# Layer 3 of a four-layer kernel on one core: delta path by channel, heads in pairs, a buffer for every group of fetched rows

## The chip, the core and the metric

The kernel runs on one core of a Trainium2 chip, as one program written by hand for five instruction streams: TensorE (PE), VectorE (DVE), ScalarE (ACT), GpSimd (POOL) and SyncE (SP), which wait for each other through semaphores. The metric is the device time of one execution in microseconds, the median of several runs. The order of each engine's instructions is what the program writes; nothing is reordered.

## What is computed

Four layers work on 4096 tokens of 128 channels (16 sequences of 256). In each, x = x + s * silu(m), where s is an attention-like part and m a feed-forward part of the normalised x. The change is in layer 3. Its s is a gated delta rule with short convolutions and three filters, four heads of 32 channels; its m is a mixture of eight experts, two for each token. Cut to what matters:

```python
b, l, d = hidden_states.shape                     # 16, 256, 128
q = _short_conv(hidden_states @ Wq.T, conv_q)     # k, v_direct alike; beta = sigmoid(h @ Wb.T)
# _delta_rule_chunkwise, chunks of 32 tokens, q and k normalised per head:
T = solve_triangular(eye - A, eye, lower=True)    # A = tril(-(kb @ k.T), -1)
u, w = T @ vc, T @ kbc
def step(S, inp):
    q_i, k_i, u_i, w_i = inp
    attn = jnp.where(causal, q_i @ k_i.T, 0.0)
    u_adj = u_i - w_i @ S
    return S + k_i.T @ u_adj, q_i @ S + attn @ u_adj
...
o = probs[..., 0:1] * local_s + probs[..., 1:2] * local_m + probs[..., 2:3] * local_l \
    + probs[..., 3:4] * delta_out + probs[..., 4:5] * v_direct
o = _rmsnorm(o, norm_w)
s = o.reshape(b, l, H * DV) @ Wo.T
# the experts: tokens are put into slots, 1280 for each expert; then
hid = gelu(a) * g                                 # a, g = halves of inp @ W_in
out_e = hid @ W_out
y = (out_pad[e_flat, l_flat].reshape(S, K, h) * gates[..., None]).sum(axis=1)
```

## The kernel before

All arrays of activations lie by channel (128 partitions) with the tokens along the free dimension; a *group* is 512 tokens (two sequences, four tiles of 128), and there are eight. All arithmetic is in float32. A call `mm(out, lhsT, rhs)` loads `lhsT` as weights, streams `rhs`, and writes `out` in one of eight PSUM banks; the trace shows two MATMUL records for each. The partitions of `lhsT` and `rhs` are the depth of the product, the width of `lhsT` is the number of output partitions, and the width of `rhs` the number of columns that stream. In the trace a form such as `128*32 128x128` reads: weights of 128 partitions and 32 columns, 128 columns streamed.

Layer 3 (`Layer3`, from L2356) has a first part (norm, routing, values, filters, scatter of the tokens into expert slots in DRAM, SyncE and GpSimd), and then four *quarters*, each of two groups (eight tiles). Every engine walks through the same numbered slots of a quarter, `L3_PERIOD` = 48 and two more in the last, and in each slot issues what is due:

- slots 0 to 3: u and w (`tensor_uw`, copied by `scalar_uw`, L3234), 16 products each, from the blocks of the inverse in `diag`, which SyncE has loaded (`sync_inverses`, L3197).
- slots 4 to 27: the recurrence over eight chunks, three slots each (`tensor_recur`): w @ S ("w"), q @ S into `b_o` ("o"), state update ("s"), four products each; VectorE subtracts after w (L3290) and masks the state after s (L3294). "w" of a chunk needs the state of VectorE, "s" needs its u.
- slots 28 to 36: eight heads (`tensor_heads`): in slot n the scores of head n into one of two banks, then the attention of head n - 1 on top of `b_o`; VectorE masks between (`vector_causal`, L3327), two buffers `s`.
- slots 35 to 45: two mixes (`*_mix`), one bank for both: VectorE multiplies the delta output by its gate (L3371), TensorE turns it ("turn", four transposes), VectorE adds it to the sum (L3377), ScalarE squares, TensorE averages, ScalarE takes Ln and Exp, VectorE scales (L3381), TensorE applies `Wo`, ScalarE copies.
- in quarters 0 to 2, beside it: the *front* of the next quarters (projections, convolution, norm, grams of q and k), the inverse of the next quarter on VectorE, one step a slot from slot 3 to 35 (`vector_invert`, L3177 to L3182), which SyncE stores and reloads from slot 37, and 14, 13 and 13 expert *units* of 256 slots: place (L2748), up (eight products 128x256, "a" and "g"), GELU on ScalarE, product on GpSimd (L2782), down.
- in quarter 3 no front and no units, but the *join*: GpSimd gathers the two expert rows of each token of a group (`gpsimd_gather`, L2811, eight indirect DMAs) into buffers of which there are two, multiplies the second half by its gate (`gpsimd_scale`, L2821), VectorE the first; TensorE adds and turns both (`tensor_join`, eight times two products with the identity), ScalarE applies SiLU (L2843), VectorE multiplies by s and adds to x (L2849, L2851). SyncE stores each group of x. Joins stand in slots 13, 17, ..., 41.

GpSimd's order in quarter 3 is gathers of groups 0 and 1, then for each group g: multiply g, gather g + 2; a gather waits for the join of the group that had the buffer before. TensorE's names in the trace: `weights_odd` and `weights_even` are two arenas of SBUF, `work` the third, `bank` is PSUM.

## Time and profile before

| | us |
|---|---|
| median of three runs | 3264.71 (3255.56 to 3266.56) |
| profiled execution | 3257.8 |
| its span | 3256.0 |
| TensorE busy (matmuls) | 2904.5 |
| VectorE, ScalarE, GpSimd busy | 1845.5, 1332.1, 1428.2 |
| layer 3, the four quarters, from the first u | 160.2, 162.0, 143.6, 150.6 |

A time of the profiled execution counts from the start of its span. Busy shares are averages over four layers with different limits. The quarters start at 2639.64, 2799.86, 2961.89 and 3105.40 us. The profile also gives the TensorE clock that was granted: 1.0 is 2.4 GHz, 0.5 is 1.2 GHz, and a mean lies between.

### The profile page before, as it was taken

What the parts mean: (1) busy time and instruction counts of PE and PEld (TensorE: products, weight loads), DVE (VectorE), ACT (ScalarE), POOL (GpSimd) and SP (SyncE); (2) the same over time, 40 slices, a digit from 0 to 9 for tenths busy, and PEclk for the clock granted to TensorE, in tenths of its full rate; (3) what the DMA queues carried; (4) which work ended last, traced back from release to release, by engine and by line L of the source; (5) the groups of instructions that cost most, each with busy time, mean ns of one, the idle gap of its engine ahead of it and who ended that gap; (6) DMA issues with size and microseconds to landing.
All of it is one profiled execution on the core that took longest, in us unless ns stands there. A gap on an engine that the chain in (4) does not pass through costs nothing.

```text
span 3256.0 us, 38772 instructions
## 1 busy us (share of the span) xinstructions
PE 2904.5 (89%) x13864; PEld 1786.7 (55%) x13864; DVE 1845.5 (57%) x3075; ACT 1332.1 (41%) x3233; POOL 1428.2 (44%) x1348
## 2 busy tenths in 40 slices
PE   6897799999999999799999999999788969898867
PEld 3564355555555555445555555444377857676756
DVE  6868577677677676466656565443442536252513
ACT  4452433433443443345555555443612323434311
POOL 3324366676676676267777777000003401010144
PEclk8997899999999999799999999999777768787876
DMA  5451100000000000420000000221121111111111
GB/s 187 159 177 55 50 1 1 1 1 1 1 1 1 1 1 1 102 63 15 1 1 1 1 1 1 66 75 56 40 82 59 56 35 41 46 36 48 37 39 46
DMA packets 160928, 128.88 MB, mean 40 GB/s; under 512 B 97688, under 2 KB 136864, under 8 KB 160224
## 3 DMA queue, kind: packets, MB, share of 16 engines
q1 hardware_dynamic: 148832, 90.13, 9.9%
q0 software_dynamic: 11904, 36.27, 3.5%
q8 instruction: 111, 1.82, 0.2%
q14 instruction: 81, 0.66, 0.1%
HBM read 105.70 MB, written 38.47 MB: 44 GB/s over the span
## 4 chain that ended last, share of the span: by engine, by line
PE 48%; ACT 4%; DVE 3%; issue 2%; POOL 1%; another core or an unknown queue 1%; SPq 0%; DMA 0%; DVEq 0%; ACTq 0%
PE bank L63 43%; PE bank L2051 4%; POOL weights_odd L2782 1%; SPq L3197 0%; ACT L3104 0%; DVE work L3179 0%; DVE work L3177 0%; DVE work L3136 0%; PE bank L2748 0%; PE bank L2901 0%; DVE weights_even L3136 0%; DVE work L1984 0%; ACT L3356 0%; POOL weights_odd L2811 0%
## 5 line engine op out<-in xcount | busy, mean ns | idle before, releaser
L63 PE MATMUL bank<-work 64*128 64x256 f32 (+5 forms) x4384 | 623.2, 356 | 16.9 <-DVE work L3294 3.9
L1491 POOL TENSOR_TENSOR work<-work 128x512 f32<-128x512 f32 x384 | 494.4, 1288 | 320.6 <-DVE work L1483 303.5
L63 PEld LDWEIGHTS bank<-work 64*128 64x128 f32 (+4 forms) x4384 | 444.6, 179 | 240.1 <-issue 135.6
L2039 POOL TENSOR_SCALAR work<-work 128x256 f32<-128x256 f32 x512 | 463.7, 922 | 242.2 <-DVE work L2030 242.0
L63 PE MATMUL bank<-weights_odd,normed_channels 128*128 128x512 f32 (+3 forms) x1152 | 524.8, 563 | 23.0 <-DVE work L1483 16.2
L63 PE MATMUL bank<-work,weights_even 128*32 128x128 f32 (+4 forms) x1136 | 326.3, 462 | 50.0 <-issue 10.6
L2024 ACT ACTIVATE work<-bank,work 128x256 f32<-128x256 f32 x512 | 236.8, 474 | 194.8 <-DVE work L2010 190.7
L1483 DVE TENSOR_TENSOR work<-bank,work 128x512 f32<-128x512 f32 x360 | 245.5, 686 | 110.0 <-PE bank L63 106.6
L63 PEld LDWEIGHTS bank<-weights_odd,normed_channels 128*128 128x128 f32 x1152 | 183.8, 195 | 161.1 <-issue 80.2
L63 PEld LDWEIGHTS bank<-work,weights_even 128*32 128x32 f32 (+4 forms) x1136 | 149.3, 180 | 184.0 <-issue 131.2
L2782 POOL TENSOR_TENSOR weights_odd<-weights_odd 128x512 f32<-128x512 f32 x40 | 51.5, 1288 | 445.1 <-ACT weights_odd L2777 445.1
L2010 DVE TENSOR_REDUCE work<-bank 128x2 f32<-128x512 f32 x256 | 164.9, 686 | 132.3 <-PE bank L63 132.3
L63 PE MATMUL bank<-work,weights_odd 128*128 128x512 f32 (+3 forms) x520 | 209.4, 519 | 25.5 <-ACT work L3355 6.6
L1558 ACT ACTIVATE work<-bank,work 128x256 f32<-128x256 f32 x256 | 119.6, 473 | 274.9 <-DVE work L1545 274.8
L63 PE MATMUL bank<-normed_channels,weights_even 128*128 128x512 f32 x432 | 230.5, 620 | 0.8 <-DVE work L1977 0.8
L63 PE MATMUL bank<-weights_even,work 128*128 128x128 f32 (+4 forms) x1152 | 176.1, 317 | 24.1 <-DMA work<-chunk_inverses 23.3
L2051 PEld LDWEIGHTS bank<-constants,work 128*128 128x128 f32 x1024 | 122.1, 141 | 123.9 <-issue 96.6
L63 PEld LDWEIGHTS bank<-weights_even,work 128*128 128x128 f32 (+2 forms) x1152 | 163.6, 221 | 41.1 <-DMA work<-chunk_inverses 23.7
L2695 POOL DMA_INDIRECT expert_rows_in<-weights_odd,expert_slots x64 | 63.7, 995 | 256.3 <-DVE expert_slots L2661 179.9
L63 PE MATMUL bank<-weights_odd 128*128 128x128 f32 (+3 forms) x664 | 149.8, 379 | 20.2 <-POOL weights_odd L2782 15.5
L1984 DVE TENSOR_SCALAR work<-bank,weights_even 128x512 f32<-128x512 f32 x128 | 96.1, 751 | 119.2 <-PE bank L63 119.2
L2051 PE MATMUL bank<-constants,work 128*128 128x128 f32 x1024 | 157.6, 276 | 2.3 <-DVE work L2059 1.1
(306 smaller groups left out, 4520.0 us busy)
## 6 DMA issues: line engine op xcount, KB each, us to landing
work<-gate_rows_L SPq DMA_DIRECT2D x64, 256.0 KB, 3.1
filter_matrices<-in_L_filters SPq DMA_DIRECT2D x24, 512.0 KB, 8.2
work<-filter_matrices SPq DMA_DIRECT2D x16, 768.0 KB, 4.2
expert_rows_in<-in_zeros SPq DMA_DIRECT2D x8, 640.0 KB, 11.2
weights_odd<-expert_rows_in SPq DMA_DIRECT2D x40, 128.0 KB
expert_rows_out<-weights_odd SPq DMA_DIRECT2D x40, 128.0 KB
weights_even<-expert_rows_in SPq DMA_DIRECT2D x20, 128.0 KB
expert_rows_out<-weights_even SPq DMA_DIRECT2D x20, 128.0 KB
```

What stands on the lines that cost most here:

```text
L63: return pe.matmul(out, lhsT, rhs, start=first, stop=last, skip_group_check=True)
L1483: v.tensor_tensor(heads(dst), heads(self.b_prod[p % 2][:, :]), self.per_head(self.score[g % 3], tile, kind == 0, e), ALU.mult).then_inc(s[ ...
L1491: gp.tensor_tensor(self.sum_of(p), self.sum_of(p), self.product_of(p), ALU.add).then_inc(s["l1_add"], 1)
L1558: a.activation(self.p[n % 2][:, c], self.b_score[n % 2][:, c], ACT.Exp, bias=self.mx[n % 4][:, i:i + 1], accum_out=self.sums(bt)[:, h, i:i ...
L1984: v.tensor_scalar(dst[n % 2], self.b_misc[:, :], bias[:, m:m + 1], scale, ALU.add, ALU.mult).then_inc(s["l2_qk"], 1)
L2010: v.tensor_reduce(self.mx[h % 8][:, 0:2], self.b_score[n % 2][half][:, :].rearrange("p (i j) -> p i j", j=SEQ), AX.X, ALU.max, negate=True ...
L2024: a.activation(self.p[h % 6][:, c], self.b_score[n % 2][half][:, c], ACT.Exp, bias=self.mx[h % 8][:, i:i + 1], accum_out=self.sums(n, half ...
L2039: gp.tensor_scalar(p[:, c], p[:, c], self.sums(n, half, i), None, ALU.mult).then_inc(s["l2_p"], 1)
L2051: last = pe.transpose(self.b_turn[:, jc * SEQ + i * P:jc * SEQ + (i + 1) * P], self.p[h % 6][:, i * SEQ + jc * P:i * SEQ + (jc + 1) * P], ...
L2695: gp.indirect_dma_start(self.k.x_rows[:, :], to, self.stage[g % 4][:, i * P:(i + 1) * P], None).then_inc(s[f"rows_moved{g % 4}"], 16)
L2782: gp.tensor_tensor(h, h, self.factor[n % 2], ALU.mult).then_inc(self.k.sem["moe_scaled"], 1)
```

## The change

1. **Delta path by channel, gate in the queries.** In the front, TensorE spreads the delta path's gate over the 32 channels of each head (16 products of a broadcast column with the identity) and VectorE multiplies the normalised q by it ("gated q"). "o" and the attention are written with operands swapped, so that `b_o` holds channels by tokens. VectorE's gate step and the transposes of the mix fall away.
2. **Heads in pairs.** In one slot the scores of two heads are issued in turn into two banks, then the attention of the two heads before; slots 28 to 32 instead of 28 to 36.
3. **Mixes in own banks**, with the states `S` as scratch, four slots each, in slots 31 to 36.
4. **Own buffers for the rows of each group.** Gathers wait only for the end of the expert units, for quarter 2's last scores, and for the rows of group g - 4 to have landed. The second multiplication goes to ScalarE, four ACTIVATEs. Joins stand at slots 8, 13, 18, 23, 28, 33, 37, 39; the last quarter has 42 slots, 8 fewer.

```diff
-L3_PERIOD = 48
+L3_PERIODS = (48, 48, 48, 42)
+L3_JOINS = (7, 12, 17, 22, 27, 32, 36, 38)
...
+        fetched = Arena(region.tensor, region.at, units_at).ring((region.at - units_at) // GW)
...
+        fetched = fetched[0:2 * (GROUPS - 3)] + [a[:, i * GW:(i + 1) * GW] for a in (*self.kk[1:3], q0) for i in range(2)]
+        self.rows = [fetched[2 * g:2 * g + 2] for g in range(GROUPS)]
+        self.b_mix = (b[3], b[4])
...
     def gpsimd_gather(self, gp, on, g):
-        if g >= 2:
-            self.moe_done(on, "moe_mm", MOE_MM, ("join", g - 2))
+        self.done(on, "l3_rec_mm", REC_MM, QUARTERS - 2, ("score", PAIRS - 1))
+        if g >= 4:
+            self.gathered(on, g - 4)
...
-    def gpsimd_scale(self, gp, on, g):
+    def scalar_scale(self, a, on, g):
         self.gathered(on, g)
-        gp.tensor_tensor(x, x, self.gates_of(1, g), ALU.mult).then_inc(self.k.sem["moe_scaled"], 1)
+        for i in range(TPG):
+            x, t = self.rows[g][1][:, i * P:(i + 1) * P], TPG * g + i
+            last = a.activation(x, x, ACT.Copy, scale=self.gate[1][:, t:t + 1])
+        last.then_inc(self.k.sem["moe_act"], 1)
...
+        if step == 5 and (g := self.front_of(n, 0)) is not None:
+            self.wait_front(on, "l3_front_dve", FRONT_DVE.index(("gated q", g)) + 1)
+            on.wait_ge(s["l3_probs"], 36)
+            for i in range(TPG):
+                for h in range(L3_H):
+                    last = mm(pe, b[h * L3_D:(h + 1) * L3_D, i * P:(i + 1) * P], self.path_gate(g, i, h), k.ident)
+            last.then_inc(done, 1)
...
+            v.tensor_tensor(dst, dst, self.b_front[:, :], ALU.mult).then_inc(done, 1)
...
-                last = mm(pe, o[r, i * P:(i + 1) * P], q[:, at:at + L3_CHUNK], S[:, b * P:(b + 1) * P],
-                          first=c < L3_CPT and b % BPG == 0, last=False)
+                last = mm(pe, o[:, i * P + r.start:i * P + r.stop], S[:, b * P:(b + 1) * P], q[:, at:at + L3_CHUNK],
+                          first=c == 0 and b % BPG == 0, last=False)
...
     def tensor_heads(self, pe, on, quarter, n):
             for i in range(TPG):
-                t = slice(at + i * P, at + (i + 1) * P)
-                last = mm(pe, self.b_head[n % 2][:, i * P:(i + 1) * P], kk[r, t], q[r, t])
+                for e in range(2):
+                    j, h = HEADS[2 * n + e]
+                    r, t = slice(h * L3_D, (h + 1) * L3_D), slice(j * GW + i * P, j * GW + (i + 1) * P)
+                    last = mm(pe, self.b_head[e][:, i * P:(i + 1) * P], kk[r, t], q[r, t])
             last.then_inc(done, 1)
...
-                last = mm(pe, self.b_o[j][:, d], self.s[(n - 1) % 2][:, i * P:(i + 1) * P],
-                          self.u[:, j * GW + d.start:j * GW + d.stop], first=False, last=True)
+                for e in range(2):
+                    j, h = HEADS[2 * n - 2 + e]
+                    r, t = slice(h * L3_D, (h + 1) * L3_D), slice(i * P, (i + 1) * P)
+                    last = mm(pe, self.b_o[j][r, t], self.u[:, j * GW + t.start + r.start:j * GW + t.start + r.stop],
+                              self.s[e][:, t], first=False, last=True)
...
     def gpsimd(self, gp, on):
-        for g in range(GROUPS + 2):
-            if g >= 2:
-                self.gpsimd_scale(gp, on, g - 2)
-            if g < GROUPS:
-                self.gpsimd_gather(gp, on, g)
+        for g in range(GROUPS):
+            self.gpsimd_gather(gp, on, g)
```

What this does to the order of the instructions, at three places. First TensorE in quarter 2 from slot 28. Of the kernel before: `128x128` from `weights_even,work` are scores, `128x32` the attention, the rows of `weights_odd` an expert unit (x counts the calls of `mm`):

```order
L63 MATMUL bank<-weights_odd 128x256 x4
L63 MATMUL bank<-weights_even,work 128x128 x8
L63 MATMUL bank<-work 128x32 x4
L63 MATMUL bank<-weights_odd 128x128 x4
L2748 MATMUL bank<-constants,weights_odd 128x128 x2
L63 MATMUL bank<-weights_even,work 128x128 x4
L63 MATMUL bank<-work 128x32 x4
L63 MATMUL bank<-weights_odd 128x256 x4
L63 MATMUL bank<-weights_even,work 128x128 x4
L63 MATMUL bank<-work 128x32 x4
L63 MATMUL bank<-weights_even,work 128x128 x4
```
And now (`32x128` is the attention):

```order
L63 MATMUL bank<-weights_odd 128x256 x4
L63 MATMUL bank<-weights_even,work 128x128 x16
L63 MATMUL bank<-work 32x128 x8
L63 MATMUL bank<-weights_odd 128x128 x4
L2765 MATMUL bank<-constants,weights_odd 128x128 x2
L63 MATMUL bank<-weights_even,work 128x128 x8
L63 MATMUL bank<-work 32x128 x8
L63 MATMUL bank<-weights_odd 128x256 x4
L63 MATMUL bank<-weights_even,work 128x128 x8
L63 MATMUL bank<-work 32x128 x16
L63 MATMUL bank<-work,weights_odd 128x512
```
Two heads stand where one stood, the scores of two pairs come first, and the mean of the first mix follows the last attention.

Second, TensorE in quarter 3 around the last recurrence step and the first heads. `constants,weights_odd 128x128 x8` is a join. Before:

```order
L63 MATMUL bank<-constants,weights_odd 128x128 x8
L63 MATMUL bank<-work 32x128 x4
L63 MATMUL bank<-work,weights_even 128x128 x8
L63 MATMUL bank<-work 128x32 x4
L63 MATMUL bank<-constants,weights_odd 128x128 x8
L63 MATMUL bank<-work,weights_even 128x128 x4
L63 MATMUL bank<-work 128x32 x4
L63 MATMUL bank<-work,weights_even 128x128 x4
L63 MATMUL bank<-work 128x32 x4
L63 MATMUL bank<-work,weights_even 128x128 x4
L63 MATMUL bank<-work 128x32 x4
L63 MATMUL bank<-work,weights_even 128x128 x4
```
And now, up to the last-but-one join (`work,weights_odd 128x512` are means and outputs of the mixes; `constants,work` and `constants,weights_even` are joins whose rows lie in the other arenas):

```order
L63 MATMUL bank<-work,weights_even 128x128 x8
L63 MATMUL bank<-constants,weights_odd 128x128 x8
L63 MATMUL bank<-work,weights_even 128x128 x8
L63 MATMUL bank<-work 32x128 x8
L63 MATMUL bank<-work,weights_even 128x128 x8
L63 MATMUL bank<-work 32x128 x8
L63 MATMUL bank<-work,weights_even 128x128 x8
L63 MATMUL bank<-work 32x128 x16
L63 MATMUL bank<-work,weights_odd 128x512
L63 MATMUL bank<-constants,work 128x128 x8
L63 MATMUL bank<-work,weights_odd 128x512 x3
L63 MATMUL bank<-constants,work 128x128 x8
```
The heads have moved together and the joins lie ahead of them and behind; before, three joins came after this place, each in front of two heads' work or of the mixes.

Third, GpSimd at the end of its stream. Before, with the expert products (L2782) ahead:

```order
L2782 TENSOR_TENSOR weights_odd<-weights_odd 128x512 x40
L2811 DMA weights_odd<-expert_rows_out,expert_slots 128x128 x16
L2821 TENSOR_TENSOR weights_odd<-weights_odd 128x512
L2811 DMA weights_odd<-expert_rows_out,expert_slots 128x128 x8
L2821 TENSOR_TENSOR weights_odd<-weights_odd 128x512
L2811 DMA weights_odd<-expert_rows_out,expert_slots 128x128 x8
```
And now:

```order
L2510 MEMSET work 128x4096
L2799 TENSOR_TENSOR weights_odd<-weights_odd 128x512 x40
L2829 DMA weights_odd<-expert_rows_out,expert_slots 128x128 x40
L2829 DMA work<-expert_rows_out,expert_slots 128x128 x16
L2829 DMA weights_even<-expert_rows_out,expert_slots 128x128 x8
```
The multiplications between the gathers are gone, and the gathers stand in one row.

## Rows read from the trace of the kernel before

**Rows 1.** Busy time by stretch: slots 28 to 47 of quarters 0 to 2, and quarter 3.
```profile
core 0: us, PE busy (x) PEld busy (x) DVE busy (x) ACT busy (x) POOL busy (x), PEclk, DMA share, GB/s
2734.03:2799.86 65.83, 52.73 (x270) 43.23 (x269) 24.24 (x30) 22.18 (x37) 8.85 (x7) 0.82 0.18 47
2898.41:2961.89 63.48, 52.88 (x252) 43.57 (x252) 24.21 (x30) 20.00 (x33) 7.60 (x6) 0.76 0.18 46
3042.14:3105.40 63.26, 52.75 (x251) 43.64 (x251) 24.70 (x31) 20.00 (x33) 7.58 (x6) 0.76 0.13 32
3105.40:3256.00 150.60, 103.14 (x585) 87.47 (x583) 36.99 (x52) 19.29 (x26) 70.50 (x72) 0.68 0.15 43
```

**Rows 2.** Timeline of TensorE, quarter 3: start, length, operation, count, idle before and releaser.
```profile
3134.83 3.62 PE L63 MATMUL bank<-work 128*32 128x128 f32 x16 [0.78 <-DVE work L3294]
...
3140.78 1.93 PE L63 MATMUL bank<-work 128*32 128x128 f32 x16 [0.78 <-DVE work L3294]
...
3144.58 1.06 PE L63 MATMUL bank<-work 128*32 128x128 f32 x8 [0.78 <-DVE work L3294]
3145.57 2.05 PE L63 MATMUL bank<-constants,weights_odd 128*128 128x128 f32 x16
...
3189.95 3.76 PE L63 MATMUL bank<-constants,weights_odd 128*128 128x128 f32 x16 [5.82 <-issue]
...
3204.89 3.76 PE L63 MATMUL bank<-constants,weights_odd 128*128 128x128 f32 x16 [7.10 <-issue]
...
3212.42 2.07 PE L63 MATMUL bank<-work,weights_even 32*128 32x128 f32 x8
3214.42 1.92 PE L63 MATMUL bank<-work 128*128 128x32 f32 x8
```

**Rows 3.** Timeline of GpSimd, quarter 3: gathers (L2811) and multiplication (L2821).
```profile
3193.98 0.98 POOL L2811 DMA_INDIRECT weights_odd<-expert_rows_out,expert_slots  x1 [4.13 <-PE bank L63]
...
3202.77 0.95 POOL L2811 DMA_INDIRECT weights_odd<-expert_rows_out,expert_slots  x1 [0.30 <-issue]
3203.73 1.06 POOL L2821 TENSOR_TENSOR weights_odd<-weights_odd 128x512 f32<-128x512 f32 x1
3208.92 0.99 POOL L2811 DMA_INDIRECT weights_odd<-expert_rows_out,expert_slots  x1 [4.13 <-PE bank L63]
```

**Rows 4.** Timeline of ScalarE: the second u copied (L3234) in quarters 2 and 3.
```profile
2974.53 0.60 ACT L3234 ACTIVATE work<-bank 128x512 f32<-128x512 f32 x1 [6.34 <-PE bank L63]
...
3129.78 0.60 ACT L3234 ACTIVATE work<-bank 128x512 f32<-128x512 f32 x1 [13.59 <-remote]
```

**Rows 5.** Timeline of TensorE, quarter 2: w, scores, attention, expert units.
```profile
2965.59 1.94 PE L63 MATMUL bank<-work,weights_even 128*32 128x128 f32 x32
...
3047.04 1.15 PE L63 MATMUL bank<-weights_even,work 32*128 32x128 f32 x8
3048.12 1.08 PE L63 MATMUL bank<-work 128*128 128x32 f32 x8
3049.03 1.97 PE L63 MATMUL bank<-weights_odd 128*128 128x256 f32 x8
...
3101.99 2.07 PE L63 MATMUL bank<-weights_odd 128*128 128x128 f32 x8 [3.55 <-POOL weights_odd L2782]
```

**Rows 6.** Timeline of TensorE in layer 2: scores in two halves of the partitions.
```profile
1906.41 1.13 PE L63 MATMUL bank<-work 64*128 64x256 f32 x8
```

**Rows 7.** Timeline of VectorE: a mask, the inverse's last step, the last step.
```profile
3052.13 0.69 DVE L3327 TENSOR_TENSOR work<-bank,weights_odd 128x512 f32<-128x512 f32 x1 [1.43 <-PE bank L63]
...
3073.66 1.22 DVE L3182 TENSOR_TENSOR work<-work,weights_odd 128x1024 f32<-128x1024 f32 x1
...
3252.85 0.69 DVE L2851 TENSOR_TENSOR x_channels<-x_channels,work 128x512 f32<-128x512 f32 x1
```

**Rows 8.** Timeline of the queue of SyncE, quarter 2: the inverse's blocks.
```profile
3081.34 15.03 SPq L3197 DMA_DIRECT2D work<-chunk_inverses  x32
```

**Rows 9.** Timeline of ScalarE, last mixes: table load and Ln.
```profile
3237.72 1.28 ACT L3356 ACT_TABLE_LOAD   x1
3239.87 0.69 ACT L3358 ACTIVATE work<-bank,constants 128x512 f32<-128x512 f32 x1 [0.86 <-PE bank L63]
```

More of the change, by code:

```diff
@@ L3442, in tensor @@
         for quarter in range(QUARTERS):
-            for slot in range(L3_PERIOD + self.TAIL * (quarter == QUARTERS - 1)):
+            for slot in range(L3_PERIODS[quarter]):
                 if slot < 4:
@@ L3499, in scalar @@
         for quarter in range(QUARTERS):
-            for slot in range(L3_PERIOD + self.TAIL * (quarter == QUARTERS - 1)):
+            for slot in range(L3_PERIODS[quarter]):
                 if slot < 4:
@@ L3609, in sync @@
             self.sync_triangles(sp, on, quarter + 1)
[L3610 removed]
+            for slot in range(L3_PERIODS[quarter]):
                 for n, step in self.front_steps(quarter, slot):
```

168 lines of the change are left out of this document (76 added, 92 removed).

## The prediction

> **What bounds the kernel now.** I read, in this order, the busy time by stretch, then the timelines of TensorE and GpSimd in the last quarter of layer 3, then those of the other quarters. Everything outside layer 3 has the same instructions after the change, so the sum is about layer 3 alone. The table by stretch gives the last quarter 150.6 us, of which TensorE is busy 103.1 at a mean granted clock of 0.68 [rows 1]. The timelines say why. GpSimd runs one serial loop per group of rows: eight gathers of 1.25 us from 3193.98, the multiplication by the gate at 3203.73, then it waits for TensorE's join before the same buffers may be filled again; the next eight start at 3208.92, so the loop takes 14.9 us [rows 3]. TensorE stands before it: the joins at 3189.95 and 3204.89 come after 5.82 and 7.10 us of idleness, which the trace calls "issue", but both start just after a multiplication of GpSimd [rows 2, 3]. The recurrence behind a join is held back with it, though it needs only 3.80 us a chunk at 2.4 GHz (3140.78 to 3144.58) and 5.95 at 1.2 GHz (3134.83 to 3140.78) [rows 2]. In the other quarters TensorE is nearly full: in slots 28 to 47, where heads, mixes and the last expert units stand, it is busy 52.8 of 63.3 us, 52.9 of 63.5 and 52.7 of 65.8 [rows 1].
>
> **The last quarter without the serial loop.** All 64 gathers now stand in a row on GpSimd, each group with its own buffer, with nothing behind them there. They take 64 x 1.25 = 80 us; group g is there about 10 (g + 1) + 4 us after the quarter's start, the last at 84. I count from the first matmul at 3105.40.
> - u and w. As now: the second u is copied at 3129.78, 24.4 us in, where the quarter before needs 2974.53 - 2961.89 = 12.6 [rows 1, 4]. Some 11 us are lost while the first 16 gathers are issued back to back. I keep them: 25.4 us to the end of u and w.
> - Recurrence: 7.5 chunk steps between 3.80 and 5.95 us, 28 to 45, taken in the middle: 37. Four joins fall into it, 2.05 us at 2.4 GHz, 3.76 at 1.2 [rows 2], of which the 0.78 us that a step waits for VectorE anyway hides a part: 4 x 2.1 = 8.
> - Heads: four pairs. One head's scores take 1.15 us at 2.4 GHz and 2.07 at 1.2, its attention 1.08 and 1.92 [rows 2, 5]. Side by side I let a pair cost what one head did (below): 1.6 + 1.5 in the middle. A pair also waits for two masks of 0.69 us [rows 7], which a single head had behind the other head's work: 1.45. 4 x 4.55 = 18.
> - Mixes: two in a row, each matmul 1.1 to 2.1, Ln and Exp 0.69 each, table load 1.28 [rows 9], VectorE 0.75 and 0.7: about 6.5 each, 13.
> - End: two joins 2 x 2.9, SiLU 0.6, table load 1.28, two VectorE steps 1.4: 9. From the last VectorE step (3252.85 + 0.69) to the end of the span 2.5 [rows 7].
>
> 25.4 + 45 + 18 + 13 + 9 + 2.5 = 113 against 150.6: **-38**. The multiplication that moves to ScalarE is four ACTIVATEs a group; ScalarE is busy 19.3 of 150.6 us [rows 1], so it costs nothing unless it stands before Ln or SiLU in the last 30 us; then a microsecond. The gathers bind nowhere: slot 22 (group 3) comes at about 60 us, its rows at 44; slot 38 (group 7) at about 95, its rows at 84.
>
> **Heads, turn and mix in quarters 0 to 2.** Do matmuls on different parts of the array overlap? In columns, yes: 16 products with 32 output partitions each, in four places (32 records), take 1.94 us, even beside matmuls at 1.2 GHz, while four in one place (eight records) take about 1 us [rows 2, 5]. In rows: layer 2's scores, 64 partitions deep in alternating halves, take 1.13 us for eight records of 256 columns, where full-depth ones take 1.97 [rows 5, 6]. So both the scores (32 rows of another head, another bank) and the attention (now 32 output partitions a head) should go in pairs. Eight heads cost some 23 us of TensorE now, part at 1.15 + 1.08 and part at 2.07 + 1.92 [rows 2, 5]; half goes: -11.5. The two transposes of the mix go: -3. What comes back: the exposed masks, of which unit work covers a part, +3.6; and in slots 37 to 47 only expert units are left, each with its own waits for ScalarE and GpSimd (3.55 us for GpSimd at 3101.99 [rows 5]), +2.7. Net -8.2, so 63.3 becomes 55; three times: **-25**.
>
> What is late next there is the inverse of the next quarter. VectorE ends its last step at 3074.9, SyncE then issues 32 transfers from 3081.34 for 15.0 us [rows 7, 8], and u and w of the next quarter need them: with 2 us to land, 23 us from VectorE to u. Now they are there 7 us early (about 3098 against 3105.4). In the new order VectorE's part shrinks only from 33 to 30 us, since the inverse itself fills slots 28 to 35, so the floor is 30 + 23 = 53 us. It takes nothing from 55, but it allows no more than 2 us beyond it.
>
> **The gate in the queries.** Per group 16 products that spread the gate, with 32 output partitions in four places: 1.94 us [rows 5], and 0.69 of VectorE. It replaces VectorE's gate step, so VectorE is even. On TensorE it stands in slots 7 and 19, beside full work: 6 x 1.94 = 12, of which I take **+10**; two more groups before quarter 0: **+4**. Bounds: nothing where TensorE waits there, 16 for all eight.
>
> **The turned product** of queries and state is now 128 deep and wide with 32 moving columns, like the old attention: 1.08 for eight records against 1.04 to 1.06 [rows 2, 5], so nothing. The Trainium skill (TensorEngine Tiling (Array Packing), Key Properties) says that changing the tiling mode drains the engine, and the new order changes mode between w and o where the old one did not. The trace bounds it: w and o together take 1.93 us, apart 1.06 + 1.04 [rows 2]: 0.17 x 28 = 5 us at most, which would make 3221 of the sum; I take 0 and keep 5 for the range.
>
> **Sum:** -38 - 25 + 10 + 4 = -49. On the profiled execution, 3257.8, that is 3209; the median of the runs, 3264.7, is 6.9 above it, so 3264.7 - 49 = **3216**.
>
> **Rivals.**
> - The long burst of gathers goes on disturbing TensorE. For: the 11 us lost at the quarter's start, where ScalarE stood 13.59 us until 3129.78, when the burst of 16 (3107 to 3127) had just ended [rows 4]. Against: in a burst of eight, from 3208.92, scores and attention keep their 2.07 and 1.92 [rows 2, 3]. If the same share is lost all along, 11 of 20 us, the burst of 80 costs 44 us, 33 more than in the sum: 3249.
> - **It stands still until the burst ends** (slower than before): u and w end at 88 us rather than 25, and everything follows: 113 + 63 = 176, +25 instead of -38, total 3279. The point that decides: more than 38 us of stalls inside the 80 us burst eat the whole gain of this quarter, and 49 that of the change.
> - The pairs don't do what they say. For the attention the overlap in columns is shown; that of 32-row parts stands in no row, and without it the scores give back half, 6 us a quarter in all four: 3240. If neither overlaps, 11.5 x 3 + 12 = 47 comes back: 3263, no change.
> - Quarters 0 to 2 gain nothing in the tail because the clock falls or the inverse is late. With only expert units in slots 37 to 47 TensorE is half idle; a unit's matmuls, 3.5 us at 2.4 GHz (1.97 of it in its largest group [rows 5]), take nearly twice that at 1.2: three units in three quarters, +27, 3243. The Trainium skill (TensorE: Matmul & The Clock Gate, Part 1) says that the throttled clock is the default and activity releases it, which speaks for this; the 0.76 of the present, busier stretch [rows 1] speaks for it too, though weakly.
>
> **How the numbers follow.** Forecast 0.53; the share lost all along 0.15; standstill 0.08; no overlap 0.09, of which neither 0.05; idle clock or late inverse 0.15. Own range of the forecast: the last quarter between 100 (clock mostly 2.4 GHz, no loss in u and w) and 123, the rest between -25 and -3: 3190 to 3235. To hold 8 in 10 it is widened to the idle clock and the share lost all along: 3188 to 3248. A measurement of this kernel can tell 0.3%, 9.8 us. Faster by more: the forecast, the share lost, the idle clock and the scores alone, 0.53 + 0.15 + 0.15 + 0.04 = 0.87; within: neither overlaps, 0.05; slower: standstill, 0.08.
>
> **What would show it.** Right: no idle time of TensorE before joins; 64 gathers in 80 us with no gap; chunk steps of 4 to 6 us; a pair of scores (16 records) in 1.2 to 2.1 us; slots 28 to 47 in some 55 us; the last quarter in 100 to 123. Wrong: ScalarE or VectorE waiting ten us and more for a matmul that the trace shows as finished, while gathers are issued; 16 records of scores in 2.2 or more at 2.4 GHz; u of the next quarter waiting for the transfers of the inverse; a granted clock near 0.5 in slots 37 to 47.

## The result, and the profile after

The kernel after took 3297.07 us in the median of four executions (3281.92 to 3304.83), the kernel before 3260.14 us beside it: a ratio of 1.0108, 95% interval 1.0063 to 1.0153. It is **slower by 1.1%**; the forecast was 3216 with a range of 3188 to 3248. The profiled execution has a span of 3280.1 us.

The table by stretch of the kernel after, with the columns of [rows 1] (first slots 28 to 47 of quarters 0 to 2, then quarter 3), shows both halves of the result:

```profile
2733.50:2795.51 62.01, 42.79 (x253) 31.21 (x253) 23.52 (x28) 22.16 (x37) 8.85 (x7) 0.79 0.19 49
2895.68:2949.74 54.06, 37.83 (x235) 27.74 (x235) 23.52 (x28) 20.19 (x33) 7.59 (x6) 0.81 0.21 52
3035.66:3089.66 54.00, 37.85 (x235) 27.73 (x235) 24.01 (x29) 20.20 (x33) 7.59 (x6) 0.81 0.15 37
3089.66:3280.10 190.44, 102.84 (x569) 82.89 (x568) 33.36 (x50) 26.96 (x57) 60.62 (x64) 0.60 0.12 34
```

Slots 28 to 47 take 62.0, 54.1 and 54.0 us against 65.8, 63.5 and 63.3 [rows 1]: 22.5 us gained. Quarter 3 starts at 3089.66 and not at 3105.40, so 15.7 us are won by then. It then takes 190.4 us against 150.6: 39.8 us lost, and the span is 24.1 us longer. Quarter 0 of the kernel before starts with its first u at 2637.27, not at 2639.64, and takes 162.6 us; that of the kernel after starts at 2638.07.

The timelines of TensorE, its weight loads (PEld), GpSimd and ScalarE in quarter 3 of the kernel after say where the time goes:

```profile
3089.66 6.87 PE L63 MATMUL bank<-weights_even,work 128*128 128x32 f32 x32
...
3107.08 1.10 PE L63 MATMUL bank<-work,weights_even 128*32 128x128 f32 x4 [1.27 <-issue]
...
3155.55 0.37 PE L63 MATMUL bank<-work,weights_even 128*32 128x128 f32 x1 [2.43 <-issue]
3158.35 0.37 PE L63 MATMUL bank<-work,weights_even 128*32 128x128 f32 x1 [2.43 <-issue]
...
3172.35 0.21 PE L63 MATMUL bank<-work 128*128 128x32 f32 x1 [2.43 <-issue]
3175.15 0.21 PE L63 MATMUL bank<-work 128*128 128x32 f32 x1 [2.59 <-issue]
...
3182.99 2.07 PE L63 MATMUL bank<-work,weights_even 32*128 32x128 f32 x8
```
```profile
3154.15 0.13 PEld L63 LDWEIGHTS bank<-work,weights_even 128*32 128x32 f32 x1 [2.67 <-issue]
3156.95 0.13 PEld L63 LDWEIGHTS bank<-work,weights_even 128*32 128x32 f32 x1 [2.67 <-issue]
```
```profile
3092.89 1.01 POOL L2829 DMA_INDIRECT weights_odd<-expert_rows_out,expert_slots  x1 [5.15 <-issue]
...
3171.78 0.95 POOL L2829 DMA_INDIRECT weights_even<-expert_rows_out,expert_slots  x1 [0.30 <-issue]
```
```profile
3104.99 0.60 ACT L3269 ACTIVATE work<-bank 128x512 f32<-128x512 f32 x1 [7.82 <-remote]
3168.16 0.60 ACT L3269 ACTIVATE work<-bank 128x512 f32<-128x512 f32 x1 [62.57 <-remote]
3183.06 0.60 ACT L3269 ACTIVATE work<-bank 128x512 f32<-128x512 f32 x1 [14.30 <-remote]
```

GpSimd issues its 64 gathers from 3092.89 to 3171.78 without a gap, as the change means it to. For 12 us TensorE does not notice. From 3107 it thins out, and from 3119 to 3178 it starts, with two exceptions, one matmul in 2.80 us, a matmul of 128 moving columns (0.37 us) as one of 32 (0.21 us), with idle time that the trace calls "issue": it waits for nothing that the profile shows. Before its copy of the second u ScalarE stands idle for 62.57 us. At 3183, some 10 us behind the last gather, everything is back at its pace. u and w thus end 93 us after the quarter's start and not 25. This comes nearest to the rival "it stands still until the burst ends" (chance 0.08), which gave 88 us for them and 3279 in all; but TensorE does not stand still, it goes at a small fixed rate.

### The profile page after: what moved, and what is told of

The parts are those of the page before. It is cut to its first block and busy times, and to the rows that moved or that the text cites. A ratio compares the mean times of both kernels' runs of the same rounds, so it can differ in the third digit from the quotient of the medians.

```text
span 3280.1 us, 39191 instructions
## 1 busy us (share of the span) xinstructions
PE 2875.4 (88%) x14056; PEld 1752.0 (53%) x14056; DVE 1845.2 (56%) x3075; ACT 1336.7 (41%) x3264; POOL 1417.5 (43%) x1340
## 5 line engine op out<-in xcount | busy, mean ns | idle before, releaser
L63 PE MATMUL bank<-work 64*128 64x256 f32 (+5 forms) x4384 | 593.6, 354 | 33.0 <-issue 11.4
L63 PEld LDWEIGHTS bank<-work 64*128 64x128 f32 (+4 forms) x4384 | 413.7, 173 | 256.6 <-issue 145.7
L63 PE MATMUL bank<-work,weights_even 32*128 32x128 f32 (+4 forms) x1008 | 310.1, 485 | 95.4 <-issue 61.4
L63 PEld LDWEIGHTS bank<-work,weights_even 32*128 32x128 f32 (+4 forms) x1008 | 132.7, 189 | 229.7 <-issue 185.1
L1558 ACT ACTIVATE work<-bank,work 128x256 f32<-128x256 f32 x256 | 119.1, 471 | 275.3 <-DVE work L1545 275.2
L63 PE MATMUL bank<-work,weights_odd 128*128 128x512 f32 (+3 forms) x520 | 208.6, 517 | 24.5 <-ACT work L3136 5.7
L63 PE MATMUL bank<-weights_even,work 128*128 128x32 f32 (+4 forms) x1280 | 195.8, 319 | 32.2 <-DMA work<-chunk_inverses 23.7
L63 PEld LDWEIGHTS bank<-weights_even,work 128*128 128x128 f32 (+2 forms) x1280 | 182.0, 225 | 50.3 <-DMA work<-chunk_inverses 24.1
## 6 DMA issues: line engine op xcount, KB each, us to landing
expert_rows_in<-in_zeros SPq DMA_DIRECT2D x8, 640.0 KB, 11.6
```

The source lines that it names most:

```text
L63: return pe.matmul(out, lhsT, rhs, start=first, stop=last, skip_group_check=True)
L1558: a.activation(self.p[n % 2][:, c], self.b_score[n % 2][:, c], ACT.Exp, bias=self.mx[n % 4][:, i:i + 1], accum_out=self.sums(bt)[:, h, i:i ...
```

## The experiments

**Two kinds of chips.** The first surprise was not a kernel but a chip. On chip 11 (the first set of runs) the kernel before took 3229.5 us and nothing stalled, neither at the 64 gathers nor where the profile before shows ScalarE idle for a matmul at the scatters of layer 3's start (14.09 us until 2477.75 there). Chips 15 and 3 behaved like it; chips 5 and 9 like the one of the first measurement. So each comparison below names its chip, and the unchanged kernels were run on one of each kind. Each of these five chips was used for one set of runs only, so whether it is the chip or the occasion that decides is not told apart; "kind of chip" stands for both below.

Kernels before and after, unchanged, on chip 5:

> The kernel before, unchanged, once more with a profile, on the chip of these runs. In the second set of runs nothing stalled at the scatters of layer 3, where the profile of before shows ScalarE 14.09 us idle until 2477.75, and the kernel before took 3229 us and not 3260. If the stalls of TensorE during rows of gathers and scatters belong to some chips or executions and not to others (theory F), this profile shows none where the copies at the start are not held up, with 3220 to 3240 us, or shows all of them with 3255 to 3265.

> The kernel after, unchanged, timed beside the kernel before on the same chip. Theory F: where the kernel before shows no stalls, the kernel after shows none either, its last quarter takes 116 to 122 us and not 190, and the time is 0.985 to 0.992 of that of before (3180 to 3200 against 3229). Where before shows them, the ratio is 1.005 to 1.015 again. Theory A, that the row of 64 gathers stalls TensorE wherever it runs: 190 us for the last quarter in any case.

Measured: c_before 3271.38 us in its profile, c_after 3290.37 (ratio 1.0112, interval 1.0074 to 1.0149), quarter 3 184.7 us. The first result stands again, stall included; only c_before is slower than the 3255 to 3265 us expected.

And on chip 3:

> The kernel before, unchanged, with a profile on the same chip. Where nothing stalls, the last quarter is shorter than the 150.6 us of the first profile by about the 11 us lost there at its start: 138 to 142 us; the start of layer 3 comes some 15 to 20 us earlier. Where it stalls: 150 us.

> The kernel after, unchanged, once more. If this chip is one where ScalarE's copies in layer 3's start are held up (as on chips 5 and 9): last quarter 185 to 192 us, ratio 1.005 to 1.016. If it is one where they are not (as on 11 and 15): last quarter 116 to 122 us, ratio to before 0.984 to 0.992, which is the forecast of the prediction with its -49 us or a little less.

Measured: c2_before 3228.78 us, c2_after 3199.44 against 3230.80, **ratio 0.9898, interval 0.9863 to 0.9933: the same change is 1.0% faster here.** Quarter 3 of c2_before and of c2_after, by stretch:

```profile
3090.06:3227.00 136.94, 96.54 (x585) 84.82 (x583) 36.24 (x52) 19.27 (x26) 70.65 (x72) 0.71 0.16 48
```
```profile
3076.72:3195.80 119.08, 95.86 (x569) 82.24 (x568) 33.31 (x50) 26.96 (x57) 61.99 (x64) 0.64 0.19 55
```

Without stalls the quarter takes 119.1 us; the 13.7 us between 136.9 (a little less than expected) and the 150.6 of [rows 1] are the stall that the kernel before has at its own first 16 gathers, as far as one profile of each can tell. Theory F (it depends on the chip or the execution) holds; theory A in its plain form (64 gathers stall TensorE anywhere) falls. The timeline of TensorE of c2_after, beside the same gathers at the same 1.25 us:

```profile
3076.72 6.87 PE L63 MATMUL bank<-weights_even,work 128*128 128x32 f32 x32
3083.52 1.94 PE L63 MATMUL bank<-work,weights_even 128*32 128x128 f32 x32
3085.39 7.04 PE L63 MATMUL bank<-weights_even,work 128*128 128x32 f32 x32
3092.36 1.94 PE L63 MATMUL bank<-work,weights_even 128*32 128x128 f32 x32
3094.22 1.92 PE L63 MATMUL bank<-work 128*128 128x32 f32 x8
```

**Whose gathers, whose stall.** Plain loads in place of gathers (`gp` is here the stream of SyncE, which now calls this function; the waits that count the landed rows are adapted):

```diff
-                gp.indirect_dma_start(self.rows[g][which][:, i * P:(i + 1) * P], None, self.k.y_rows[:, :],
-                                      of).then_inc(s[f"rows_moved{g % 4}"], 16)
+                gp.dma_start(self.rows[g][which][:, i * P:(i + 1) * P], self.k.y_rows[t * P:(t + 1) * P, :]).then_inc(
+                    s[f"places_landed{g % 3}"], 16)
...
+        for g in range(GROUPS):
+            self.gpsimd_gather(sp, on, g)
```

> The kernel after, with the 64 gathers replaced by 64 plain loads of the same size and shape from the same table in HBM, issued by SyncE (consecutive rows in place of the chosen ones, so the mixture of experts comes out from other rows). The same bytes come at about twice the rate. If the gathers hurt because GpSimd issues them with a row list (theory A), TensorE runs through: last quarter 100 to 120 us, time 3200 to 3215. If the traffic into SBUF as such hurts (theory C), TensorE stalls for as long as the loads last, some 40 us: 3240 to 3260.

> The kernel after with the 64 gathers replaced by 64 plain loads of the same size issued by SyncE (consecutive rows in place of the chosen ones), again, since nothing stalled where it ran before. Where the copies at the start of layer 3 are held up: theory A (the gathers of GpSimd are what holds TensorE) gives 117 to 122 us for the last quarter, theory C (traffic into SBUF) 140 and more.

Measured: on chip 11 3183.61 us, quarter 3 118.8 us, which tells nothing, as nothing stalled there. On chip 9, where the copies at the start of layer 3 are held up (12.47 us), the same kernel took 3225.91 us and its quarter 3:

```profile
3105.32:3224.10 118.78, 95.60 (x569) 81.95 (x568) 33.26 (x50) 26.96 (x57) 0.00 (x0) 0.64 0.18 55
```

The same bytes, issued in 31 us in place of 79 (SyncE issues from 3107.84 to 3139.20), cost nothing, while the kernel after with a probe (e3b_probe, below) stalls on the same chip. Theory C (traffic into SBUF) falls; it is the gathers of GpSimd. (The edit changes two things at once, the kind of transfer and the engine that issues it; they are not told apart.)

Added work on the other two engines (ScalarE's stream first, then VectorE's):

```diff
+                if quarter == QUARTERS - 1 and slot == 1:
+                    for i in range(64):
+                        a.activation(self.silu[1][:, 8 * i:8 * i + 8], self.k.const[:, 0:8], ACT.Copy)
...
+                if quarter == QUARTERS - 1 and slot == 5:
+                    self.gathered(on, 0)
+                    for i in range(80):
+                        v.tensor_reduce(self.silu[0][:, 4 * i:4 * i + 4], self.k.const[:, 0:4 * P].rearrange("p (a b) -> p a b", a=4), AX.X, ALU.add)
```

> The kernel after, with added work that nothing reads: VectorE does 80 reductions of 512 columns (0.69 us each undisturbed) once the first group of rows has landed, ScalarE 64 small ACTIVATEs of 8 columns behind the first copy of w. Both fall into the stretch where TensorE starts one matmul in 2.80 us. If only TensorE's instructions are held back (theory D), the reductions follow each other at 0.69 us and the ACTIVATEs at about 0.2 us, and the time stays within 10 us of 3297. If every instruction of every engine is (theory E, what they write out together is limited), VectorE and ScalarE also slow down, to 2.8 us an instruction at worst, and TensorE is slower still or the stall longer.

> The kernel after with added work that nothing reads, now so placed that it holds nobody up where TensorE stalls: VectorE does 80 reductions of 512 columns (0.59 us each in the second set of runs) behind the clearing of the state, ScalarE 64 ACTIVATEs of 8 columns (0.10 us each there) behind the first copy of w. Where TensorE stalls: theory D (only TensorE's instructions are held back) lets both run at these rates in the middle of the stall; theory E (what all engines write out is limited) slows them down to between 1 and 3 us each. Where nothing stalls it only delays the quarter by some 45 us.

The first of the two (chip 11, VectorE's part in slot 0, where it held up the clearing of the state) took 3229.98 us and shows the undisturbed pace: 80 reductions in 47.56 us, 64 ACTIVATEs in 6.40 us. On chip 9 e3b_probe took 3298.13 us; its timelines of VectorE, ScalarE and TensorE:

```profile
3117.39 25.14 DVE L3566 TENSOR_REDUCE work<-constants 128x4 f32<-128x512 f32 x42 [39.05 <-DMA weights_odd<-expert_rows_out,expert_slots]
3143.25 0.69 DVE L3566 TENSOR_REDUCE work<-constants 128x4 f32<-128x512 f32 x1 [0.71 <-issue]
3144.65 0.69 DVE L3566 TENSOR_REDUCE work<-constants 128x4 f32<-128x512 f32 x1 [0.71 <-issue]
```
```profile
3116.38 2.06 ACT L3511 ACTIVATE work<-constants 128x8 f32<-128x8 f32 x20
...
3141.14 0.21 ACT L3511 ACTIVATE work<-constants 128x8 f32<-128x8 f32 x1 [1.19 <-issue]
3142.54 0.21 ACT L3511 ACTIVATE work<-constants 128x8 f32<-128x8 f32 x1 [1.19 <-issue]
```
```profile
3141.86 0.37 PE L63 MATMUL bank<-work,weights_even 128*32 128x128 f32 x1 [2.43 <-issue]
3144.66 0.37 PE L63 MATMUL bank<-work,weights_even 128*32 128x128 f32 x1 [2.43 <-issue]
```

This is the key reading. VectorE runs 42 reductions at 0.60 us, ScalarE 20 ACTIVATEs at 0.10 us; then each of them gets **one instruction in 1.40 us**, whatever the instruction's own length (0.69 and 0.21 us). TensorE's 2.80 us are the same figure: each of its matmuls comes with a weight load, and the two alternate at 1.40 us (matmul at 3155.55 between the weight loads at 3154.15 and 3156.95). And TensorE is no slower with the other two at work than without. So theory D (only TensorE) falls and theory E holds in part: each of the three engines is limited, each to its own one instruction in 1.40 us, once something that first absorbs some tens of instructions is full. GpSimd's own gathers keep their 1.25 us on both kinds of chip. An engine with many short instructions, as TensorE here, suffers most.

What this limit is the runs don't show. Every execution here, a timed one too, comes with a record of its instructions. The Trainium skill (NOTIFIC — the notification-queue block, 7.1, "Overflow: three behaviours, one of which stalls the engine", and 10, "Constraints, capacities, measured rates") says that the unit that writes such records out can hold some 500 of them inside and lets the producers wait rather than lose one there. That a full store of records is what holds the engines here is an inference. The order of events fits: a free start, then an equal limit for each engine, then 10 us behind the last gather to recover. One store that all engines share does not fit: VectorE runs at full pace until 3142.5, 24 us after TensorE (3118) and ScalarE (3118.7) are held back. Section 10 also puts the cost of a record to the engine at zero; if the inference holds, the 2.80 us stand against that. No run here is without records, so whether the change is slower on such a chip when nobody records stays open, as does what tells the chips apart.

**Pauses.** Each group's gathers wait until the rows of the group before have landed:

```diff
-        if g >= 4:
-            self.gathered(on, g - 4)
+        if g >= 1:
+            self.gathered(on, g - 1)
```

> The kernel after, with one edit: GpSimd issues the gathers of a group only when the rows of the group before have landed, so eight gathers stand together and a pause of some 2 to 3 us follows. If an unbroken row of gathers is what holds TensorE back (theory A), its stalls of 2.4 us between single matmuls are gone or short, the last quarter is set by 8 groups of about 12.5 us and falls from 190.4 us to 115 to 130, and the time to 3210 to 3225. If any stream of gathers does it, pauses or not (theory B, a share of the time that gathers are in flight), the pauses give back only their own 20 us: 3265 to 3285.

> The kernel after with the gathers of a group held until the rows of the group before have landed, again, now beside the unchanged kernel after on one chip. Where before shows stalls: theory A and F, the last quarter 115 to 130 us against 190, 60 us faster than c_after. Where it shows none: the same as c_after within 5 us, since 64 gathers are far from binding.

Measured: on chip 11 3198.62 us, ratio 0.9901 (0.9870 to 0.9933), quarter 3 118.8 us. On chip 5 3247.12 us, ratio 0.9956 (0.9929 to 0.9982), quarter 3 139.8 us: 43 us better than c_after in the median, where 60 were expected, but 21 us of stall remain, in u and w (to 3131) and in the two chunks behind them, where VectorE's step comes late and TensorE stands 7.17 us:

```profile
3124.51 0.64 PE L63 MATMUL bank<-work,weights_even 128*32 128x128 f32 x4 [0.35 <-issue]
...
3139.75 3.76 PE L63 MATMUL bank<-work 128*32 128x128 f32 x16 [7.17 <-DVE work L3330]
```

From 3160 on the gathers go on as before, and TensorE stands no longer than in c2_after (2.70 us at most, for ScalarE). The expectation of 115 to 130 us was too good; a pause of 1.8 us in 11.6 is not enough while TensorE does the 64 products of u and w (128 records; the expectations call them products) in 18 us.

Waiting for the join two groups back (`self.moe_done(on, "moe_mm", MOE_MM, ("join", g - 2))` for g >= 2 in place of the same two lines), which is the order of the kernel before with own buffers:

> The kernel after, with one edit: the gathers of group g wait for the join of group g - 2, as in the kernel before; own buffers, gates on ScalarE and everything else stay. The first 16 gathers still stand in a row, the others come in eights. Theory A: the start loses about the 11 us that the kernel before lost, and the rest is as there with the join two groups behind: the last quarter 130 to 145 us, time 3225 to 3240. Theory B: 3260 and more.

> The kernel after with the gathers of group g held until the join of group g - 2, again. Where TensorE stalls: the first 16 gathers meet u and w as in the kernel before and cost the same 11 us, the others come in eights beside thinner work: 125 to 140 us for the last quarter, ratio to the kernel before 0.988 to 0.997. Where nothing stalls: 120.6 us again, ratio 0.989.

Measured: chip 11 3192.15 us, ratio 0.9891 (0.9844 to 0.9939), quarter 3 120.6 us; chip 9 3249.80 us, ratio 0.9963 (0.9945 to 0.9982), quarter 3 141.5 us, just outside the 125 to 140 expected. The first 16 gathers cost u and w the usual 10 us. The others did not come in eights: those of two groups stand in a row from 3144.30 to 3164.9, with the second long wait of TensorE (7.10 us, to 3163.54) in it, and three groups from 3173.82 to 3206.7 with pauses under 2 us, with a third (6.30 us, to 3209.82) behind them.

**Late gathers.** The wait of e1_land, and one more:

```diff
+        if g >= 1:
+            self.gathered(on, g - 1)
+            self.done(on, "l3_uw_mm", UW, QUARTERS - 1, ("w", GPQ - 1))
```

> The kernel after with the gathers of a group held until the rows of the group before have landed, and from group 1 on also until TensorE has issued the last product of u and w, so that its densest stretch (128 products in 18 us) meets eight gathers only. Where TensorE stalls (chip 5, in the third set of runs): a backlog that the dense stretch fills and a thinner one drains (theory H) gives 118 to 128 us for the last quarter, against 139.8 with the pauses alone, and a ratio to the kernel before of 0.985 to 0.992. If pauses of 2 us are simply too short, whatever stands beside them (theory B), the same 140 us, ratio 0.996. Where nothing stalls: 119 to 125 us.

> The kernel after with each group's gathers held until the rows of the group before have landed, and from group 1 on until u and w are issued, once more, as the partner of e11_nogate and on another day of the chips. Ratio to the kernel before 0.990 where TensorE stalls (0.9899 on chip 9), 0.985 to 0.992 where it doesn't; last quarter 119 to 124 us in both.

Measured: chip 9 3227.95 us against 3261.52, ratio 0.9899 (0.9874 to 0.9925); chip 15 3190.16 against 3225.59, ratio 0.9884 (0.9838 to 0.9930). Quarter 3 takes 122.3 us on chip 9 and 118.9 on chip 15. On chip 9 u and w run through:

```profile
3103.38 6.87 PE L63 MATMUL bank<-weights_even,work 128*128 128x32 f32 x32
3110.18 1.94 PE L63 MATMUL bank<-work,weights_even 128*32 128x128 f32 x32
3112.05 7.04 PE L63 MATMUL bank<-weights_even,work 128*128 128x32 f32 x32
3119.02 1.94 PE L63 MATMUL bank<-work,weights_even 128*32 128x128 f32 x32
```

Theory H fits and theory B falls: from 3121.73 on the gathers come in eights with pauses of 1.8 us, and no stall follows. A backlog that the densest stretch fills and thinner work drains explains that; the pause behind the first eight is also longer here (5.34 us), and no run parts the two. The two waits on GpSimd turn +1.1% (chip 5 and the first) into -1.0% (chip 9) where the kernel stalls and cost nothing measurable where it doesn't. This version is faster than the kernel before on both kinds, and, by these ratios, than the kernel after where that stalls.

**An even, slower rate.** Four tiny operations of GpSimd behind each gather:

```diff
+                for n in range(4 * (8 * g + TPG * which + i), 4 * (8 * g + TPG * which + i + 1)):
+                    gp.tensor_scalar(self.factor[1][:, 2 * n:2 * n + 2], self.k.ident[:, 0:2], 1.0, None, ALU.mult)
```

> The kernel after with four tiny operations of GpSimd (128 x 2, results unused) behind each gather, so that the 64 gathers stand at even distances of some 1.7 to 2.0 us in place of 1.25, with no pause between groups; the last rows then come at 110 to 130 us and set the end. If the rate decides (theory I), TensorE runs freely between gathers at the slower pace, and a stall is short or missing where c_after had one. If only a longer pause lets the engines recover (theory J), one matmul in 2.80 us as before, and the last quarter 190 us and more. Where nothing stalls at all, 125 to 140 us by the gathers alone.

> The kernel after with the 64 gathers at even distances of 1.94 us (144.1 us for the last quarter where nothing stalled, set by the gathers alone). Where TensorE stalls in c2_after: theory I (the rate decides) gives 144 to 150 us for the last quarter and no or short waits of TensorE; theory J (only a pause lets the engines recover) one matmul in 2.80 us until the gathers end at about 130 us, then the rest: 210 us and more. Where nothing stalls: 144 us again.

Measured: 3217.72 us on chip 15 and 3230.51 on chip 3, quarter 3 144.1 and 143.8 us, set by gathers at 1.94 us each (the first expectation, 125 to 140, was too good). Neither chip stalls, so whether the rate or the pause spares the engines stays open.

**Heads in pairs.** The four products of one head, then the four of the other, for scores and attention:

```diff
-            for i in range(TPG):
-                for e in range(2):
+            for e in range(2):
+                for i in range(TPG):
```

> The kernel after, with the order of the products inside a pair changed: first the four of one head, then the four of the other, for scores and attention, in place of one head's and the other's in turn. The products are the same, only neighbours now use the same part of the array. If it is the alternation that lets two heads overlap (theory G), a pair takes twice as long: 16 records of scores 2.2 us at 2.4 GHz and 4 at 1.2 and as much for the attention, 8 to 12 us more in each quarter, 30 to 45 us in all. If the array does not overlap them anyway, or overlaps them in any order, nothing changes.

Measured on chip 5: 3310.90 us against 3290.37 for c_after (ratios to before 1.0150, 1.0107 to 1.0193, and 1.0112). The intervals overlap, but the traces don't need them: quarters 0 to 2 take 483.0 us against 460.8 in c_after and 454.8 in e1b_land, which has the same instructions there. Pairs of e6_nopair in quarter 2, scores and attention, at 2.4 GHz, at 1.2 and at 2.4 again:

```profile
3064.03 1.71 PE L63 MATMUL bank<-weights_even,work 32*128 32x128 f32 x16
...
3075.42 3.09 PE L63 MATMUL bank<-weights_even,work 32*128 32x128 f32 x16
3078.44 2.77 PE L63 MATMUL bank<-work 128*32 128x128 f32 x16
3083.26 1.71 PE L63 MATMUL bank<-weights_even,work 32*128 32x128 f32 x16
3084.90 1.53 PE L63 MATMUL bank<-work 128*32 128x128 f32 x16
```

and of the kernel after, alternating:

```profile
3043.93 1.16 PE L63 MATMUL bank<-weights_even,work 32*128 32x128 f32 x16
3045.02 1.07 PE L63 MATMUL bank<-work 128*32 128x128 f32 x16
```

Alternating, a pair costs what one head cost, 1.16 and 1.07 against 1.15 and 1.08 [rows 5]. In blocks it costs 1.71 and 1.53, one and a half times as much and not twice. Theory G is right in kind, its 30 to 45 us were some 22 to 28.

**The gate in the queries.** On the version with late gathers, 15 of 16 products that spread the gate left out:

```diff
-            for i in range(TPG):
-                for h in range(L3_H):
-                    last = mm(pe, b[h * L3_D:(h + 1) * L3_D, i * P:(i + 1) * P], self.path_gate(g, i, h), k.ident)
-            last.then_inc(done, 1)
+            mm(pe, b[0:L3_D, 0:P], self.path_gate(g, 0, 0), k.ident).then_inc(done, 1)
```

> e9b_late with 15 of the 16 products a group left out that spread the gate of the delta path (the output of that path is then multiplied by what the bank holds); VectorE's multiplication stays. The prediction's term says 1.94 us a group where TensorE is full: 10 us for quarters 0 to 2 and 4 before, 14 us less in all. If these products lie in gaps of TensorE, nothing to 5 us.

Measured on chip 15: 3187.60 us against 3190.16 for e9b_late, within noise of each other, and quarters 0 to 2 take 458.1 us without the products against 455.4 with them. Of the 14 us there is no sign, but a part of them can't be excluded. The same instructions took 451.6 us in quarters 0 to 2 of after and 460.8 in c_after, and 118.9 us in quarter 3 of e9b_late and 111.3 in e11_nogate, at a granted clock of 0.64 and 0.70. In the trace of the kernel after one group's products stand in TensorE's stream for 1.5 us (2671.90 to 2673.37), between other work:

```profile
2672.25 1.12 PE L63 MATMUL bank<-constants,weights_odd 128*32 128x128 f32 x27
```

Six groups are 9 us of TensorE at 2.4 GHz; how much of it the other waits hid these runs don't say.

## Why the prediction was wrong

**The step that failed** is the first line of the last quarter: "Some 11 us are lost while the first 16 gathers are issued back to back. I keep them: 25.4 us to the end of u and w." It took for a fixed sum what grows with the row of gathers. The 13.59 us of [rows 4] were what 16 gathers cost; 64 in a row cost, on the same kind of chip, 93.4 us to the end of u and w: 68 more. That alone turns -49 into about +19, and the profiled execution moved by +24.

**The rival was there, and the argument against it was the wrong one.** Against a lasting disturbance stood that scores and attention keep their 2.07 and 1.92 us in a burst of eight [rows 2, 3]. A backlog explains that: eight gathers beside thin work did not fill what 16 gathers beside u and w filled. The evidence for the standstill was as good: ScalarE came free at 3129.78, just behind the end of the burst of 16 (3127), and not 11 us into it, so a disturbance that ends with the burst was the plainer reading of [rows 4]. Its price, 3279, is the nearest to the median of 3297, still 18 us short, 14 of them in the quarter (176 us for 190). A chance of 0.08 was far too low.

**What was right, by its steps.**
- Own buffers free the quarter of its serial loop. Without the stall (c2_after) no join is preceded by "issue", as 5.8 to 7.1 us were in [rows 2], and the quarter takes 119.1 us, inside the 100 to 123 of the forecast's own range. Point by point: u and w 17.5 us, for 25.4; the recurrence from 3094.22 to 3146.54 52.3, for 45; heads 21.5 (to 3168.02), for 18; mixes and end 27.8, for 24.5. The joins are what the sum had wrong. There are eight of them, and it counts six: four in the recurrence and two at the end. Those that stand among the heads and the mixes (slots 28 and 33) are in no term and take 3.1 and 3.2 us. The four in the recurrence take 14.2 us for 8, since most of it ran at 1.2 GHz. Without the joins the rest is as forecast: steps 38 for 37, heads 18.4 for 18, mixes and end 24.6 for 24.5 (2.70 us of it a join's wait for ScalarE's new multiplication, for which the sum had a microsecond). Of c2_after, a join in the recurrence and these two:

```profile
3102.50 3.76 PE L63 MATMUL bank<-constants,weights_odd 128*128 128x128 f32 x16
...
3148.49 3.18 PE L63 MATMUL bank<-constants,weights_odd 128*128 128x128 f32 x16 [0.79 <-DVE weights_odd L2846]
...
3172.65 3.36 PE L63 MATMUL bank<-constants,work 128*128 128x128 f32 x16 [2.70 <-ACT work L2840]
```
- Slots 28 to 47: -22.5 us for -25; 54.0 and 54.1 us in quarters 1 and 2 for 55, but 62.0 in quarter 0. The floor, the inverse, did not bind: SyncE had issued its last transfer at 3084.1, 5.6 us ahead of the next quarter's first matmul.
- The idle clock came, and the mean hides it. Slots 28 to 47 have 0.79 to 0.81, for 0.76 to 0.82 before [rows 1], but the pairs ran near 1.0 and the expert units alone behind them at 0.56, 0.66 and 0.66. The last 24.5 us of quarter 2, after and before, with the columns of [rows 1]:

```profile
3065.19:3089.66 24.47, 15.64 (x53) 11.55 (x52) 0.61 (x2) 6.89 (x12) 3.79 (x3) 0.66 0.24 54
```
```profile
3081.00:3105.40 24.40, 15.82 (x68) 11.02 (x67) 3.77 (x6) 14.70 (x22) 3.78 (x3) 0.92 0.18 33
```

  Eight records of 256 columns take 3.42 and 3.78 us there, for 1.99 at 2.4 GHz, and the first u of quarters 1 and 2, still at 1.2 GHz, 6.87 us each for 5.42 and 3.77 before. The rival's mechanism was there, but its +27 us were too much: these slots still gave 22.5 us of 25.
- The pairs overlap, scores included, for which no row stood.
- The turned product was not free: w and o together take 2.07 us (c2_after, at 3132.51), for 1.93 [rows 2], 4 us in 28 steps, near the 5 kept for the range. Whether the new form or a change of mode costs it the runs don't tell.
- The gate in the queries was taken at +14. Slots 0 to 27 of quarters 0 to 2 took 95.4 + 100.2 + 85.9 us for 96.8 + 98.6 + 80.3, so 5.9 more, of which 4.5 are the first u at the lower clock, and quarter 0 starts 0.8 us later. e11_nogate finds no sign of the 14, which were too much; between nothing and some 9 us the runs don't decide.

**On a chip that does not stall** the change brings 31 us (3230.8 to 3199.4), not 49. By parts: quarter 3 gives 17.8 us (136.9 to 119.1) where the sum had 38. Of these 20 us, 14 are the terms behind u and w, taken too small (101.6 us measured, 87.5 in the sum), 12.5 of them the joins, and 6 are stall: the 150.6 us of before hold 13.7 of it, the 113 of the sum only 8. The quarters before gave 9.3 us, where the sum had 25 - 10 = 15, and quarter 0 starts 4.0 us earlier, where the sum had 4 later: 13.3 us for 11, by luck as far as the parts go.

## What to carry to other kernels

A queue of transfers that "binds nowhere" on its own engine can still bind the others: when work that was broken up by waits becomes one unbroken row, look at what the longest such row in the old trace did to engines that share nothing with it, and extrapolate by its rate and not by its sum. Idle time called "issue" between single matmuls, or a wait for a matmul that the trace shows as long finished, is that sign. Count every instruction group that stands in a stretch before summing it; two joins of eight were in no term here. A mean clock over a stretch can hide that one part of it rose and another fell. A change of 1% should be timed on more than one chip: this one is +1.1% or -1.0% by the kind of chip alone, and waits that keep the row out of the densest stretch make it -1.0% on both.

## What the runs showed of the hardware

- On some chips (5, 9 and the first) a long row of GpSimd's gathers limits each of TensorE, VectorE and ScalarE to one instruction in 1.40 us (2.80 us for weight load and matmul), after some tens of instructions at full pace (42 of VectorE, 20 of ScalarE); it ends about 10 us behind the last gather. On others (11, 15, 3) the same code shows none of it. The kernel before takes 3260 us on the first kind and 3229 on the second: of the 29 us between the profiles before and c2_before, 15.2 lie ahead of quarter 0, where ScalarE waits at the scatters, and 13.7 in quarter 3, at its own first 16 gathers.
- Plain loads of the same bytes, issued by SyncE at more than twice the rate, cause none of it (e2b_sync on chip 9, quarter 3 118.8 us).
- Two heads on different 32-row or 32-column parts of the array overlap fully when their products alternate (16 in 1.16 us, where eight take 1.15), and in part when they stand in blocks of four (1.71 us, where two heads one behind the other would take 2.30).
